# A graph-transformer block on one Trainium2 core: the one-hots' column numbers move into PSUM, and TensorE's spare products move behind logits and one-hots

## The reference, cut to what matters

```python
N, E, HEADS = 6250, 100000, 4          # nodes, edges (sorted by dst), heads of 64
def gat_conv(x, src, dst, W, a_src, a_dst, b):
    h = (x @ W).reshape(-1, H, C)
    alpha_s, alpha_d = einsum('nhc,hc->nh', h, a_src), einsum('nhc,hc->nh', h, a_dst)
    e = leaky_relu(alpha_s[src] + alpha_d[dst], 0.2)
    m = segment_max(e, dst); ex = exp(e - m[dst]); s = segment_sum(ex, dst)
    return segment_sum(h[src] * (ex / s[dst])[:, :, None], dst) + b
xn = layernorm(x)
x = x + gnn(xn)        # gat_conv, relu, gat_conv; edges plus one loop per node
      + mix(xn)        # linear attention, 8 heads of 64
x = x + moe(layernorm(x))   # 16 experts, best 2, hidden 512, then a layer norm
```

## Time and profile before

| | |
|---|---|
| median of 3 runs | 2938.16 us (2934.69 to 2940.9) |
| profiled execution | 2947.23 us, its span 2945.6 us |
| mean granted TensorE clock in it | 0.951 of full speed |
| busy share of the span | PE 78%, POOL 67%, DVE 62%, ACT 31% |

### The profile page before, as it was taken

How to read it: one execution, slowest core, us unless ns; L and a number is a source line. 1 busy time by engine, 2 the same in 40 slices (tenths; PEclk the granted TensorE clock), 3 DMA queues, 4 the chain that set the end, 5 groups by cost and what they waited for, 6 DMA issues and landing times. The chain is left out here.

```text
span 2945.6 us, 56016 instructions
## 1 busy us (share of the span) xinstructions
PE 2306.1 (78%) x12223; PEld 1818.2 (62%) x12224; DVE 1827.1 (62%) x4382; ACT 925.0 (31%) x2254; POOL 1959.0 (67%) x1934
## 2 busy tenths in 40 slices
PE   1737887878788787728888888888888749999996
PEld 0525555555555555526666666766676539999984
DVE  5655666666666666556666666666666574555545
ACT  0512333333333333301222222222222224444445
POOL 0357777777777777557777777777777406666654
PEclk9969999999999999969999999999999879999998
DMA  3734555555555555345555555555555355565555
GB/s 69 228 102 134 140 139 138 137 138 142 141 139 141 137 137 141 88 152 154 156 150 155 149 153 149 160 148 154 150 155 150 95 149 98 103 107 102 102 90 182
DMA packets 274989, 401.59 MB, mean 136 GB/s; under 512 B 91136, under 2 KB 187799, under 8 KB 274905
## 3 DMA queue, kind: packets, MB, share of 16 engines
q0 software_dynamic: 102496, 253.89, 34.7%
q1 hardware_dynamic: 128745, 101.18, 13.2%
q10 hardware_dynamic: 43680, 45.76, 4.8%
HBM read 346.42 MB, written 54.62 MB: 136 GB/s over the span
## 5 line engine op out<-in xcount | busy, mean ns | idle before, releaser
L949 POOL DMA_INDIRECT gathered<-table,idx x1568 | 1591.8, 1015 | 506.6 <-issue 438.2
L1275 PE MATMUL psA_e<-scaled,hotf 128*128 128x260 f32 x3136 | 748.1, 392 | 67.6 <-issue 62.9
L1275 PEld LDWEIGHTS psA_e<-scaled,hotf 128*128 128x128 f32 x3136 | 588.9, 193 | 159.2 <-issue 74.1
L1249 PE MATMUL psA_e<-mixM,ident 128*128 128x256 f32 x1372 | 348.0, 391 | 91.4 <-DVE hotf L1019 85.2
L1249 PEld LDWEIGHTS psA_e<-mixM,ident 128*128 128x128 f32 x1372 | 254.0, 193 | 153.9 <-issue 122.9
L1144 ACT ACTIVATE scaled<-t_e 128x32 f32<-128x32 f32 x196 | 45.0, 230 | 807.6 <-DVE t_e L1015 801.6
L1688 POOL DMA_INDIRECT moe_d<-xscaled,xtarget x113 | 179.4, 1587 | 122.9 <-DVE xtarget L1632 52.0
L1019 DVE TENSOR_TENSOR hotf<-iota,code_r 128x1024 f32<-128x1024 bf16 x196 | 240.7, 1228 | 0.0
L1026 DVE TENSOR_TENSOR scaled<-gathered,psDW_e 128x2048 f32<-128x2048 f32 x98 | 223.8, 2283 | 25.5 <-ACT psDW_e L1145 25.5
L1026 DVE TENSOR_TENSOR scaled<-gathered,psW_e 128x2048 f32<-128x2048 f32 x98 | 223.7, 2283 | 22.0 <-ACT psW_e L1145 21.5
L1013 DVE TENSOR_TENSOR z_e<-both_e,gathered 128x32 f32<-128x32 f32 x196 | 38.2, 195 | 312.7 <-DMA gathered<-table,idx 302.6
(11 more groups left out here) (319 smaller groups left out, 3186.4 us busy)
## 6 DMA issues: line engine op xcount, KB each, us to landing
w<-codes_d SPq DMA_DIRECT2D x196, 256.0 KB, 3.7
gathered<-table,idx POOLq DMA_INDIRECT x1584, 3.3
w<-in_L_ffn_w ACTq DMA_DIRECT2D x8, 2048.0 KB, 19.6
xb<-in_L_ffn_b SPq DMA_DIRECT2D x113, 128.0 KB
table<-acc POOLq DMA_DIRECT2D x49, 130.0 KB
table<-acc ACTq DMA_DIRECT2D x49, 130.0 KB, 2.3
xnT_d<-xnT ACTq DMA_DIRECT2D x49, 128.0 KB, 1.8
w<-xnT_d SPq DMA_DIRECT2D x49, 128.0 KB, 3.7
```

What stands on the lines that cost most here:

```text
L949: pool.indirect_dma_start(out=G[:, q, k, :], out_offset=None, in_=table, in_offset=bass.IndirectOffsetOnAxis(ap=idx[:, q, k:k + 1], axis=0 ...
L1249: pe.matmul(psA[:, q, 0:C], ident[:], idle_rhs, start=True, stop=True)
L1275: ins = pe.matmul(psA[:, q, 0:GW], hotf[:, q, k, :], scaled[:, par, k, :], start=(k == 0), stop=(k == KT - 1))
```

## The change

The column numbers are copied once per stage into columns 384 to 511 of each of the three `psA_e` banks, in fp32, by three DVE copies at the head of DVE's program. `placed` reads them there instead of from `iota`. PE may not write a bank while DVE reads it, so the spare products that ran while rows were being gathered are taken out; in the second stage two others are put in behind the logits, and these go to columns 256 to 511 of the bank of `psD_e`, which now has a bank of its own. The products behind the one-hots stay. All eight gathers of a slot count on one semaphore, where there were two.

```diff
@@ gat_edges: banks
-            psD = pb("psD_e", [P, 2 * KT, 3, H])
+            psD_bank = pb("psD_e", [P, 512])
+            psD = psD_bank[:, 0:6 * KT * H].rearrange("p (k c h) -> p k c h", c=3, h=H)
@@ POOL
             def gather_rows(q):
                 for k in range(KT):
                     pool.indirect_dma_start(out=G[:, q, k, :], out_offset=None, in_=table,
-                                            in_offset=bass.IndirectOffsetOnAxis(ap=idx[:, q, k:k + 1], axis=0)).then_inc(s[f"g_half{q}" if 2 * k < KT else f"g_in{q}"], 16)
+                                            in_offset=bass.IndirectOffsetOnAxis(ap=idx[:, q, k:k + 1], axis=0)).then_inc(s[f"g_in{q}"], 16)
...
-            for landed in (s["g_half0"], s["g_in0"]):
-                hold(pool, landed, rounds * (8 * KT * FIRST) + 8 * KT, s["tick"])
+            hold(pool, s["g_in0"], rounds * (16 * KT * FIRST) + 16 * KT, s["tick"])
@@ DVE
             dve.sem_inc(s["hotT"], 2)
+            for q in range(SLOTS):
+                dve.tensor_copy(psA[:, q, 512 - P:512], iota[:]).then_inc(s["columns"], 1)
             dve.tensor_copy(mark[:], partition[:]).then_inc(s["pass"], 1)
...
             dve.wait_ge(s["own_terms"], H)
+            dve.wait_ge(s["columns"], SLOTS)
...
             def edge_logits(g, c, q, par, use):
...
-                dve.wait_ge(s[f"g_half{q}"], 8 * KT * use + 8 * KT)
-                dve.wait_ge(s[f"g_in{q}"], 8 * KT * use + 8 * KT)
+                dve.wait_ge(s[f"g_in{q}"], 16 * KT * use + 16 * KT)
...
             def placed(g, c, q, par, use):
                 dve.wait_ge(s["added"], g + 1)
-                dve.tensor_tensor(hotf[:, q, :, :], iota[:].rearrange("p (k f) -> p k f", k=1).to_broadcast([P, KT, P]),
+                dve.tensor_tensor(hotf[:, q, :, :], psA[:, q, 512 - P:512].rearrange("p (k f) -> p k f", k=1).to_broadcast([P, KT, P]),
                                   code_r[:, ds(c * KT, KT)].rearrange("p (k f) -> p k f", f=1).to_broadcast([P, KT, P]), ALU.is_equal).then_inc(s["hotf"], 1)
@@ PE
-            def while_gathered(landed, n):
-
-                def step(g, c, q, par, use):
-                    pe.wait_ge(s["acc"], g * 2 + 2)
-                    pe.wait_ge(s[f"{landed}{q}"], 16 * KT // 2 * use + 16 * KT // 2)
-                    spare_products(q, n)
-                return step
-
             def after_logits(g, c, q, par, use):
                 pe.wait_ge(s["logits"], g + 1 + SLOTS)
+                if not attention:
+                    for _ in range(2):
+                        pe.matmul(psD_bank[:, 256:256 + C], ident[:], mixM[:, 0, :], start=True, stop=True)
...
-                chunks(pe, nothing, nothing, (1, targets), (2, add), (7, fin_turn, True), (7, dots, True), (8, project, True), (1, while_gathered("g_half", 1)),
+                chunks(pe, nothing, nothing, (1, targets), (2, add), (7, fin_turn, True), (7, dots, True), (8, project, True),
                        (1, after_logits), (5, keys, True), (4, values, True), (1, after_placed(2)))
...
-                chunks(pe, nothing, nothing, (1, targets), (2, add), (12, gates, True), (10, fin_turn, True), (1, while_gathered("g_half", 2)), (7, mix, True),
-                       (1, while_gathered("g_in", 2)), (1, after_logits), (1, after_placed(3)))
+                chunks(pe, nothing, nothing, (1, targets), (2, add), (12, gates, True), (10, fin_turn, True), (7, mix, True),
+                       (1, after_logits), (1, after_placed(3)))
```

More of the change, by code:

```diff
@@ L150, in build @@
     weights_in = nc.alloc_semaphore(name="weights_in")
-    firsts = [(nc.alloc_semaphore(name=f"ahead{l}_idx_in0"), nc.alloc_semaphore(name=f"ahead{l}_g_half0"), nc.alloc_semaphore(name=f"ahead{l}_g_in0")) for l in range(2)]
+    firsts = [(nc.alloc_semaphore(name=f"ahead{l}_idx_in0"), nc.alloc_semaphore(name=f"ahead{l}_g_in0")) for l in range(2)]
     with ExitStack() as top:
@@ L583, in _ @@
                 pool.indirect_dma_start(out=G[:, 0, k, :], out_offset=None, in_=table,
-                                        in_offset=bass.IndirectOffsetOnAxis(ap=idx[:, 0, k:k + 1], axis=0)).then_inc(ahead[1 + 2 * k // KT], 16)
+                                        in_offset=bass.IndirectOffsetOnAxis(ap=idx[:, 0, k:k + 1], axis=0)).then_inc(ahead[1], 16)
         @block.vector
@@ L840, in gat_edges @@
             one = sb("one", [P, NT])
-        names = ["idx_in1", "idx_in2", "g_half1", "g_half2", "g_in1", "g_in2", "codes_in0", "codes_in1", "hotT", "hotf", "targets", "dwin", "own", "own_weights",
+        names = ["idx_in1", "idx_in2", "g_in1", "g_in2", "codes_in0", "codes_in1", "hotT", "hotf", "targets", "dwin", "own", "own_weights",
                  "own_terms", "target_read", "logits", "weights", "scaled", "added", "acc", "pass", "dests", "dest_steps", "vsteps", "logit_steps", "tick",
-                 "nears", "constants", "rden", "hidden", "fin_turned", "end"]
+                 "nears", "columns", "constants", "rden", "hidden", "fin_turned", "end"]
         if attention:
@@ L850, in gat_edges @@
         s = {n: sem(f"g{layer}_{n}") for n in names}
-        s["idx_in0"], s["g_half0"], s["g_in0"] = ahead
+        s["idx_in0"], s["g_in0"] = ahead
         FIRST = len(range(0, NC, SLOTS))
@@ L1008, in edge_logits @@
                 dve.wait_ge(s["targets"], g + 1)
-                dve.tensor_reduce(both[:], (psD if attention else psD[:]).rearrange("p k c h -> p k h c"), AX.X, ALU.add).then_inc(s["target_read"], 1)
+                dve.tensor_reduce(both[:], psD.rearrange("p k c h -> p k h c"), AX.X, ALU.add).then_inc(s["target_read"], 1)
                 dve.wait_ge(s["target_read"], g + 2)
-                dve.wait_ge(s[f"g_half{q}"], 8 * KT * use + 8 * KT)
-                dve.wait_ge(s[f"g_in{q}"], 8 * KT * use + 8 * KT)
+                dve.wait_ge(s[f"g_in{q}"], 16 * KT * use + 16 * KT)
                 logit.link(dve.tensor_tensor(z[:], target, G[:, q, :, C:GW], ALU.add))
@@ L1266, in step @@
                     pe.wait_ge(s["hotf"], g + 1)
-                    spare_products(q, n)
+                    for _ in range(n):
+                        pe.matmul(psA[:, q, 0:C], ident[:], wext[:, 0, 0:C] if attention else mixM[:, 0, :], start=True, stop=True)
                 return step
```

## The result

| | before | after |
|---|---|---|
| median | 2938.49 us of 4 runs (2934.69 to 2940.9) | 2850.94 us of 4 runs (2849.36 to 2856.6) |
| profiled execution | 2947.2 us, span 2945.6 us | 2856.6 us, span 2855.0 us |
| mean granted TensorE clock in it | 0.951 | 0.939 |

The ratio is 0.9699, with an interval of 0.9684 to 0.9714: 87.5 us less, where 78 were forecast. The forecast of 2860 us is 9 us too high, and the time lies within its range.

A forecast was written before the change was run, and what follows sets the result against it. POOL's row of gathers was taken as the bound. One-hots -85.0, `hotT` +5 and copies +1.8 made -78 us, 2869 from the profiled 2947.2, or 2860 us on the runs' median; range for 8 in 10: 2844 to 2890 us.

The forecast's parts named there:

- The bound: Both edge stages: POOL's row of gathers sets the pace, 10.50 and 10.45 us per chunk of eight, and everything else follows.
- The one-hots' 85.0 us: Both stages: 148 gathers held behind one-hots with two SBUF operands; the PSUM operand removes all 85.0 us (bounds 0 and 85.0).
- The rival of no change: Long gathers have a third cause or the one-hot holds by what it writes; 85 us stay, time 2938; chance 0.05.
- `hotT`: Behind the one-hot, `hotT` still holds gathers; out of step it costs 8 to 18 us against today's 8, so +5 us.
- The second rival: POOL and DVE fall in step, each `hotT` meeting a gather at half its length: 47 us lost, time 2894; chance 0.07.
- One sign of being wrong: In the edge stages, gathers now standing behind `hotT` by 0.2 us or more would show the prediction wrong.
- The copies: Three DVE copies at each stage's head, 0.9 us, ahead of L990, delay POOL's row: +1.8 us for two stages (1.2 to 2.2).
- The one-hot's own time: DVE's one-hot, 1228 ns: an operand in PSUM costs 0 to 0.03 us, hidden by DVE's wait for rows.
- the cover: DVE's wait for rows, about 1.0 us per chunk left, hides the one-hot's PSUM cost; without it 6 us.
- Semaphore and spare products: One gather semaphore changes nothing; fewer spares leave PE 7.8 us per chunk in both stages, below 10.03: no time gained or lost.
- The rival on PE's clock: Fewer spares idle PE and lower its clock; below 0.75 the change loses, at 0.70 the time is 3079 us; chance 0.04.
- The profile that was foretold: Signs in both stages: chunk 10.0 to 10.15 us, one-hot 1.22 to 1.26, row wait about 1.0, mean gather near 0.96, clock above 0.9.

The follow-up runs named there:

- the last two experiments: Changed kernel with each chunk's idx loaded earlier in SP's queue: first also with own weights read from PSUM, 2842.41 us; then without that, 2856.28 us.
- the two edits together: Changed kernel with own weights read from PSUM at the stages' head and idx loaded earlier in SP's queue: 2842.41 us, ratio 0.9681.

## Why the prediction was right, step by step

**The bound.** Right. POOL's row of gathers sets the pace: the gathers' own 90.3 us are the spans' difference, and fewer of them save time at once.

**The one-hots' 85.0 us.** Right in size and cause: none of the 180 gathers inside one-hots takes over 0.96 us. With the operand alone put back the hold is back, with the same 0.82 us from the one-hot's end to the gather's. Of the two rules of the Trainium skill that the prediction weighed (SBUF — State Buffer, section Who interferes with whom), the one on two SBUF inputs agrees with both runs, 0.95 and 1.75 us; the inference that `tensor_tensor` doesn't stall transfers issued by GpSimd is contradicted for these gathers. Of instructions with one SBUF input the Trainium skill says it only outside the modes that take both of DVE's ports, a condition that the prediction left out and that matters for `hotT`. The rival of no change, that the hold comes with what the one-hot writes, falls with that experiment, whose output is the same.

**`hotT`.** This term was mis-sized: +5 us forecast, but it holds 40 gathers for 4.8 us where it held 91 for 8.0. The prediction also missed a second kind of meeting: gathers that start within `scaled`, 0.4 to 0.5 us ahead of the next `hotT`, end 0.12 us behind that `hotT`. These were 30 for 1.7 us before, and are 12 for 0.9 now. Together `hotT` gave 4 us. I took the engines as out of step and the meetings as random, and chose the middle of 8 and 18. The second rival, 47 us, was refuted with it. The 9 us between +5 and -4 are the greatest part of what the sum missed, 78 against 87.5 by the medians and 90.6 by the profiled spans. One sign of being wrong was there: 5 gathers stand 0.2 us or more behind `hotT` (1 before), too few to matter. In the last two experiments the same `hotT` costs more, in an unchanged loop, so the size of this term hangs on the phase, which I had no way to read ahead of the run.

**The copies.** The three take 0.68 us, not 0.9. But L992 starts 1.1 us later than L990 did (184.90 against 183.78), and its five held gathers lose 10.9 us instead of 9.9. The term was +1.8 us for both stages; that 1.0 us is what the held gathers show of it.

**The one-hot's own time.** Right: 1222 ns against 1228, so no cost, and the cover was not needed.

**Semaphore and spare products.** Right in that they cost nothing. PE's work per chunk is 659.27 / 83.75 = 7.87 us in the first stage (7.8 forecast). In the second it is 688.85 / 81.75 = 8.43, more than the 7.8 forecast; the clock of 0.94 would by an estimate make 7.8 / 0.94 = 8.3 of it. The rival on PE's clock did not come about: at 0.83, with fewer spares still, PE needs 607.96 / 81.75 = 7.4 us of the 10.03.

**The profile that was foretold.** Chunk 10.0 to 10.15: 10.03. One-hot 1.22 to 1.26: 1.22. Wait for rows about 1.0 us: 0.93 and 1.19. Mean gather of the stages 0.96: 0.958. Clock above 0.9: 0.99 and 0.94.

**What is left.** All 1,584 gathers together went from 1607.7 us to 1517.1, the 90.6 of the spans. In it, -85.0 for the one-hots, -4.0 for `hotT` and +1.0 for L992 make -88.0. Most of the other 2.6 is in gathers that nothing holds: those of at most 0.958 us had a mean of 948.2 ns before and have 946.8 now, 2.3 us over all. No run tells why; in the six experiments that mean is 945.3 to 945.8, and 2 us are below what a measurement of this kernel tells from no change.

## What to carry to other kernels

When an engine that is never kept waiting issues the same operation a thousand times, compare its longest with its median, and look at what another engine runs during the long ones; here an end that always came 0.82 us behind a DVE operation's end named the cause. Here an operation that read one of its two operands from PSUM took no longer (1222 ns against 1228), and let the gathers pass. Before freeing such a wait, look for the one behind it: at the stage's head it was an index load that stood in SP's queue behind a load of something else, and only the two edits together gained.

## What the runs showed of the hardware

- The same two-operand operation, 1.23 us long in both, cost 85.0 us of longer gathers in one kernel and 95.5 in another, by where the gathers' starts fell in it. Whoever measures such a hold in one kernel has it to some 10 us for another.
- Not only operations with two SBUF tensors hold gathers. `hotT` reads a tensor and one column per partition from SBUF, for 0.48 us, and a gather that meets it waits for its end as well (timeline of the changed kernel):

```profile
322.76 0.48 DVE L1004 TENSOR_SCALAR hotT<-w,mark 128x1024 bf16<-128x1024 int16 x1
322.89 1.16 POOL L950 DMA_INDIRECT gathered<-table,idx  x1 [0.30 <-DVE scaled L1028]
```

  The hold ends at 323.24, the gather 0.81 us later. `hotT` handles its 1,024 elements in 0.48 us where the one-hot needs 1.22. The Trainium skill (SBUF — State Buffer, section Who interferes with whom) has `tensor_scalar` among the operations that can run in a faster mode that takes both of DVE's ports and then blocks GpSimd; the pace and the hold agree with it, though no run here tells which mode it was.
- The hold works the other way too. This gather of the changed kernel starts 0.48 us ahead of a `hotT` and takes its usual time; `hotT` takes 0.72 us where it mostly takes 0.48, and ends 0.25 us behind the gather:

```profile
463.41 0.95 POOL L950 DMA_INDIRECT gathered<-table,idx  x1 [0.30 <-issue]
...
463.89 0.72 DVE L1004 TENSOR_SCALAR hotT<-w,mark 128x1024 bf16<-128x1024 int16 x1
```

  So it goes with 31 of the 196 `hotT` of the changed kernel, for 4.4 us of DVE's time (3 of 196 before). DVE had that to spare.
- A granted clock of 0.83 instead of 0.94 over 820 us, with fewer products for PE, changed nothing in a stage whose bound is elsewhere (654 gathers in both).
